# Attention keys stacked by 4 transfers per batch in place of 16

## The reference

```
x = x + attention(layernorm(x), ctx, ctx, mask, W_q, W_k, W_v, W_o)
    q, k, v = Q @ W_q.T, K @ W_k.T, V @ W_v.T          # 16 heads of 8 columns
    scores  = clip(q k^T / sqrt(8), -50, 50)
    attn    = exp(scores) / sum(exp(scores))            # over 1444 keys
    out     = (attn v) @ W_o.T
x = x + experts(layernorm(x), gate_w, w1, w2)           # 8 experts, top 2 of each row
```

## Time and profile before

| what | value |
|---|---|
| median of 3 runs | 1222.54 us (1222.02 to 1223.01) |
| profiled execution | 1220.12 us, of which its span is 1218.4 us |
| PE busy | 1074.9 us, 88% of the span |
| DVE, ACT, POOL busy | 860.4, 753.7, 366.9 us |
| transfers on q1 | 152.55 MB, 54.3% of 16 engines' span |
| of these, into `k_stack` | 512 transfers of 192 KB |

### The profile page before, as it was taken

How to read it: one execution, slowest core, us unless ns; L and a number is a source line. 1 busy time by engine, 2 the same in 40 slices (tenths; PEclk the granted TensorE clock), 3 DMA queues, 4 the chain that set the end, 5 groups by cost and what they waited for, 6 DMA issues and landing times.

```text
span 1218.4 us, 30948 instructions
## 1 busy us (share of the span) xinstructions
PE 1074.9 (88%) x10734; PEld 778.3 (64%) x10735; DVE 860.4 (71%) x1955; ACT 753.7 (62%) x959; POOL 366.9 (30%) x357
## 2 busy tenths in 40 slices
PE   5699999999999999999999999999999999869990
PEld 3466666666666666666666666666666666569990
DVE  4567777777777777777777777777777777644443
ACT  2576666666666676766666766666666666634440
POOL 3712222222222222222222222222222222235554
PEclk8799999999999999999999999999999999979995
DMA  6655666666555665555555556666666666312225
GB/s 157 144 125 137 143 146 145 145 144 139 133 131 135 145 145 135 134 134 134 134 134 134 132 133 138 145 145 145 145 145 137 134 135 141 113 48 66 68 57 162
DMA packets 89010, 159.58 MB, mean 131 GB/s; under 512 B 13792, under 2 KB 66020, under 8 KB 88980
## 3 DMA queue, kind: packets, MB, share of 16 engines
q1 hardware_dynamic: 84084, 152.55, 54.3%
q0 software_dynamic: 4896, 6.63, 2.0%
HBM read 36.83 MB, written 22.08 MB: 48 GB/s over the span
## 4 chain that ended last, share of the span: by engine, by line
PE 64%; DVE 17%; ACT 5%; issue 5%; SPq 4%; DMA 4%; ACTq 0%; DVEq 0%; POOL 0%; POOLq 0%
PE o_sum L701 17%; PE scores L689 15%; DVE probs L1047 12%; PE scratch L618 6%; PE scratch L632 6%; PE scratch L613 5%; ACT k_full L866 4%; PE scores L805 4%; PE scores L816 4%; SPq L405 3%; PE scratch L624 2%; DVE v_both L983 2%; PE scratch L662 2%; DMA k_stack<-k_lo 2%; DMA x_all<-in_x_dram 1%
## 5 line engine op out<-in xcount | busy, mean ns | idle before, releaser
L899 ACT ACTIVATE probs<-scores 128x1200 f32<-128x1200 f32 x512 | 589.5, 1179 | 114.9 <-PE scores L689 114.9
L1047 DVE TENSOR_SCALAR probs<-probs 128x1200 f32<-128x1200 f32 x512 | 471.2, 947 | 52.9 <-ACT probs L899 50.4
L689 PE MATMUL scores<-q_stack,k_stack 128*128 128x400 f32 x1536 | 431.3, 395 | 13.4 <-DMA k_stack<-k_lo 11.3
L689 PEld LDWEIGHTS scores<-q_stack,k_stack 128*128 128x128 f32 x1536 | 255.8, 190 | 141.6 <-issue 98.3
L701 PE MATMUL o_sum<-probs,v_both 128*17 128x200 f32 x6144 | 309.8, 334 | 0.1
L701 PEld LDWEIGHTS o_sum<-probs,v_both 128*17 128x17 f32 x6144 | 154.8, 97 | 84.1 <-issue 16.5
L632 PE MATMUL scratch<-w_turned,ctxT 128*128 128x128 f32 x768 | 112.0, 289 | 56.0 <-DVE logits L1100 41.3
L570 POOL DMA_INDIRECT expert_rows<-rows,row_atu x64 | 79.0, 1235 | 264.0 <-DVE row_atu L1140 238.2
L632 PEld LDWEIGHTS scratch<-w_turned,ctxT 128*128 128x128 f32 x768 | 93.8, 192 | 87.3 <-DVE logits L1100 51.3
L505 POOL TENSOR_TENSOR q_stack<-q_parts,head_mask 128x1600 fp32r<-128x1600 f32 x32 | 107.4, 3357 | 96.9 <-DVE q_parts L970 96.9
L560 POOL TENSOR_SCALAR rstd<-moments 100x1 f32<-100x1 f32 x32 | 39.0, 1220 | 279.5 <-DVE moments L1085 279.5
(11 more groups left out here) (145 smaller groups left out, 869.8 us busy)
## 6 DMA issues: line engine op xcount, KB each, us to landing
k_stack<-k_hi SPq DMA_DIRECT2D x256, 192.0 KB, 4.6
k_stack<-k_lo SPq DMA_DIRECT2D x256, 192.0 KB, 5.4
expert_rows<-fill SPq DMA_DIRECT2D x32, 406.2 KB
xT_and_ctx<-in_ctx_dram SPq DMA_DIRECT2D x16, 704.0 KB
ctx_nat<-in_ctx_dram SPq DMA_DIRECT2D x16, 704.0 KB
v_both<-expert_rows SPq DMA_DIRECT2D x57, 65.0 KB, 1.8
xT_and_ctx<-in_L_ffn_w_dram SPq DMA_DIRECT2D x1, 2048.0 KB, 11.7
w_sb<-in_L_ffn_w_dram SPq DMA_DIRECT2D x8, 256.0 KB, 7.1
```

The lines of the kernel that those rows point to most:

```text
L689: last = nc.tensor.matmul(scores[:, c % 2, m, 0:GQ], k_stack[p][:, g, t * P:(t + 1) * P], q_stack[p][:, g, :, :].rearrange("p h q -> p (h ...
L899: nc.scalar.activation(probs[:, c % RING, :, :], scores[:, c % 2, :, 0:GQ], ACT.Exp, scale=SCALE).then_inc(exp_ready, 1)
L1047: nc.vector.tensor_scalar(chunk, chunk, LOW, HIGH, ALU.max, ALU.min).then_inc(probs_ready, 1)
```

## The change

The columns of the key weights are written in another order: from (group, head, column) to (head, column, group). `k_hi` and `k_lo` then hold the four groups' rows of one (head, column) next to each other, and 128 rows of 6 KB match 32 partitions of `k_stack` with 24 KB each, row for row. One transfer fills one term for all four groups. The transfers of a batch move the same bytes to the same places as before; `KD`, for which PE and DVE wait, is a quarter. ACT's copy of the turned weights becomes three copies, the first of which reorders.

```
-    KD = 16 * 4 * GROUPS
+    KD = 16 * 4
...
                 for t, part in enumerate((k_hi, k_lo, k_hi, k_lo)):
-                    for g in range(GROUPS):
-                        sp.dma_start(k_stack[p][t * R:(t + 1) * R, g, :].bitcast(F32),
-                                     part[g * R:(g + 1) * R, :].bitcast(F32)).then_inc(k_stacked, 16)
+                    sp.dma_start(k_stack[p][t * R:(t + 1) * R, :, :].bitcast(F32),
+                                 part[:].bitcast(F32)).then_inc(k_stacked, 16)
...
             act.wait_ge(w_in_psum, 1)
-            nc.scalar.copy(w_turned[:].rearrange("p n d -> p (n d)"), scores[:, 1, 2, :]
+            nc.scalar.copy(w_turned[:, WK, :].rearrange("p (h d g) -> p h d g", h=HG, d=DH),
+                           scores[:, 1, 2, WK * P:(WK + 1) * P].rearrange("p (g h d) -> p h d g", g=GROUPS, h=HG))
+            nc.scalar.copy(w_turned[:, WQ, :], scores[:, 1, 2, WQ * P:(WQ + 1) * P])
+            nc.scalar.copy(w_turned[:, WV:, :].rearrange("p n d -> p (n d)"), scores[:, 1, 2, WV * P:]
                            ).then_inc(w_turned_ready, 1)
```

## The result

| | before | after |
|---|---|---|
| median of 4 runs | 1222.28 us | 1678.22 us (1677.44 to 1679.05) |
| ratio to before | | 1.3733, 95% interval 1.3716 to 1.375 |
| profiled execution's span | 1218.4 us | 1676.4 us |

The change costs 456 us, 37%. The forecast was "no change"; rival B said 1684.

The account below looks back on a forecast made before the run. PE was taken to bound the kernel, the stack being in time by 0.2 us. Five savings of 0.3 us, 1.5 us, all else 0, took the median from 1222.54 to 1221.0 us, "no change"; range of 8 in 10: 1218 to 1248.

Parts of the forecast that it names:

- rival B: Stack transfers: the 16 engines write half as many places at a time, 105.5 GB/s; +462 us, 1684; chance 10%.
- What bounds the kernel: PE busy 1074.9 of 1218.4 us, never waiting for the stack in 26 like batches; room 0.2 us per batch.
- The rate: Stack transfers on the DMA engines: taken to stay at 211 GB/s, bounds 105.5 and 406.
- My chances: Whole kernel: no change 48%, slower by a little 24%, slower by much 10%, faster 14%, much faster stack 4%.
- Rival A: Stack transfers: reads from 128 partitions meet each other, 195 GB/s, PE waits in every batch; +24 us, 1247; chance 24%.
- SP's issues: On SP: 12 fewer per batch at 0.53 to 0.60 us each, hidden by the transfers' backlog; saved on the path 0.
- ACT's copies: On ACT: one 0.58 us copy becomes three, at most 1.7 us more, hidden by a 2.64 us wait for PE; cost 0.
- the 8.45 that the prediction had named as a sign: On ACT: if its copies mattered, the copy behind them (L847) would start after 8.45.
- Issuing the later loads sooner: On SP: table fills some 8 us and expert weights up to 7 us earlier; taken as 0, at most +5 us once.
- The 0.3 us that each stack was to save by its fewer transfers: Stack transfers: 0.025 us each beside the bytes, 12 fewer; shows at the start and in four late batches, 1.5 us.

Follow-up runs that it names:

- the deal experiment: Only transfers, 768 KB from 128 SBUF partitions, only the destination varied: 32 partitions 1, 2, 4 apart 115, 111, 413 GB/s; 64 partitions 1, 2 apart 110, 413.
- the row order alone: Changed kernel's row order and three ACT copies, but the stack filled by 16 transfers to the old places: 1509.09 us, ratio 1.2331 to the kernel before.

## Why the prediction was wrong, point by point

**What bounds the kernel: right.** The stack had 0.2 us of room in a batch, no gain was to be had in the steady batches, and everything hung on the stack's rate.

**The rate: wrong, the step that failed.** "I take 211, the nearest row: the engines are fully busy at it, and the destination, 32 partitions for each term, stays as it is." The rate was 112 GB/s. The destination as a whole did stay, and with it the number of places that the transfer covers (places in the sense of the last transfer experiment: four neighbours, and the four that are 32 further on, are one). What changed is which of them the 16 engines write at the same moment. By the deal that this experiment bears out, an engine's share of the 128 rows now starts with four neighbouring source rows, and these are the four groups of one (head, column): one partition. So the 16 engines begin on destination partitions 0 to 7 and 16 to 23 of the term, four of the 16 places, and go on to the other four of the eight. The 211 GB/s of the kernel before is the rate of eight. Counted so, the stretches at a share near 1.00 gave 95 to 115 GB/s with 4 places in use, 172 to 220 with 8 and 339 to 413 with 16.

The Trainium skill has both halves of this: SBUF — State Buffer, "Door 1: The DMA port swizzle", puts four neighbours and the four that are 32 further on one port, at about 27 GB/s a port, which 4, 8 and 16 ports at 110, 211 and 413 bear out. DMA: Bandwidth & Descriptors, "The descriptor swizzle", gives the deal of a 128-partition transfer. I used the first to cap the destination and left the second to a rival; the deal experiment agrees with it, while the DRAM source of 128 rows (207) shows that not every transfer that is written with 128 rows is dealt so.

**Rival B: the mechanism right, its terms only roughly.** It had the deal, and the half rate. Its 1684 is near 1678.22 partly by luck. It counted 14.4 us of waiting for a batch, by 105.5 GB/s; the rate was 112 and the waiting 12.0 us. What it left out is the clock: PE, made to wait, works 2.7 us longer in each batch. The two misses nearly cancel: 12.0 + 2.7 = 14.7.

**My chances: wrong.** B had 10% and lay outside the range. The argument against it ("such a deal would have to be kept where the two sides differ in partitions, which no row shows") was no evidence; absence of a row is what makes a bound, and this end was dear, 462 us against a gain of at most 10 at the other. The one row that bore on it, 406 GB/s at share 1.00 in the earlier trace rows, stood in its favour, as the prediction itself says, and was given little weight.

**Rival A: its mechanism was not seen.** Where it could be tested by itself, unlike pairs of reading and writing places cost nothing (199 and 197 against 172 and 194).

**The small steps: mostly right.** SP's issues were free. ACT's copies cost nothing: the copy behind them began at 8.57 us, later than the 8.45 that the prediction had named as a sign, but it still waited 2.47 us for PE. Issuing the later loads sooner delayed the stacks by little: the first one's last transfer landed after 27.3 us against 26.6 in a steady batch, and PE waited 12.55 us for the last stack against 11.96. The 0.3 us that each stack was to save by its fewer transfers has nothing for it: alone, at unchanged places, four transfers took 17.7 us and sixteen 17.0.

**What stays open.** With 32 source partitions four apart and 32 neighbouring destinations the rate was 145 GB/s (139 alone), between the levels for 4 and 8 places. That is the case of the row order alone, and its cost, 285 us, rests on no tested explanation. T1b would explain it (dealt by source partition, an engine's first row goes to one set of four places and its second to the other, so that the two sets mix), but that was only argued. Nor was the mirror explained (32 neighbours to 128, 179 GB/s), nor 64 to 32 neighbours (123), nor why the same pattern, 128 to 32 four apart, ran at 359 GB/s in one kernel and at 413 in another. How rows from DRAM are dealt wasn't tried beyond the two forms above.

## What to carry to other kernels

Before merging transfers, write down for each DMA engine which partitions it reads and writes at the same moment: the merge here, which put four neighbouring source rows of 128 SBUF partitions into one of 32 neighbouring destination partitions, gathered the 16 engines on a quarter of the places, and no count of partitions or bytes shows it. A transfer that is backlogged (landings growing by more than the issues) is bound by its rate, so fewer issues can't help it; and where the wait has 0.2 us of room, an unmeasured rate is the whole forecast. Interleaving what is stacked, row by row over all 128 partitions, gave 339 GB/s where blocks of 32 gave 112.

## What the hardware showed that I had not expected

- The same 128 SBUF partitions to 32 others: 115 GB/s to neighbours, 111 two apart, 413 four apart; to 64 neighbours still 110.
- Reading is limited like writing: 16 neighbours read and written four apart, 109 GB/s; 8 apart read and written to 16 neighbours, 109.
- A DMA share of 1.00 says nothing of the rate: it stood with 110 and with 413 GB/s.
- 12 us of waiting cost PE another 2.7 us, as its clock went to 0.50 and was back at about 659 us, 6 us after the wait.
